# Decoder with two cross attentions: parts of 112 and 336 columns ahead of each, a fourth token buffer, token splits in other chunks

## The reference

```python
x = ln(x + linear_attn(x))                        # layer 0
def mha(x, y):                                    # 16 heads of 32
    q = ln(x) @ wq; k = ln(y) @ wk; v = ln(y) @ wv
    a = softmax(q @ k.T * 32 ** -0.5)             # causal mask for the self attention only
    x_out = x + (a @ v) @ li1_w + li1_b
    return x_out + gelu(ln(x_out) @ li2_w + li2_b) @ li3_w + li3_b
def xattn(x, ctx):
    x = ln(x); x = x + mha(x, x); x = ln(x)       # "self attention", first MLP
    return x + mha(x, ctx)                        # "first cross attention", second MLP
x = ln(x + xattn(x, ctx)); x = ln(x + fp6_linear(x))
x = ln(x + memory_block(x))                       # layer 1; ends in a third MLP with silu
x = ln(x + cross_attn(x, ctx))                    # "second cross attention", 16 heads of 8, biased
x = ln(x + moe(x))
```

## Time and profile before

| | us |
|---|---|
| median of 3 runs | 697.91 (696.05 to 698.76) |
| the profiled execution, its own time | 696.02 |
| its span in the trace | 694.2 |
| PE busy | 642.1 (92%) |
| DVE busy | 500.0 (72%) |
| ACT busy | 336.9 (49%) |
| POOL busy | 340.4 (49%) |
| granted TensorE clock, mean | 0.999 |

### The profile page before, as it was taken

The page is one execution under the profiler, slowest core; times in us unless marked ns, Lnnn a source line. Parts: engine busy times, 40 slices in busy tenths (PEclk is TensorE's granted clock), DMA queues, the critical chain, the costliest instruction groups (busy, mean ns, idle before and its releaser), DMA issues.

```text
span 694.2 us, 20149 instructions
## 1 busy us (share of the span) xinstructions
PE 642.1 (92%) x8946; PEld 483.4 (70%) x8946; DVE 500.0 (72%) x815; ACT 336.9 (49%) x503; POOL 340.4 (49%) x256
## 2 busy tenths in 40 slices
PE   8788987999999999999998888899999999998997
PEld 4576785677777777777776567567777777776774
DVE  3666733888888888887465761878988988888443
ACT  2153465066456456454354337076466465464443
POOL 1351363087696696664220313066776766845400
PEclk9999999999999999999999999999999999999999
DMA  9600003000000000000030000000000000000000
GB/s 263 225 1 2 3 2 128 1 2 2 3 2 2 2 2 2 3 2 2 2 130 22 0 1 1 1 2 2 2 2 2 2 2 2 3 2 1 3 1 13
DMA packets 3506, 14.74 MB, mean 21 GB/s; under 512 B 372, under 2 KB 628, under 8 KB 3420
## 3 DMA queue, kind: packets, MB, share of 16 engines
q1 hardware_dynamic: 3420, 13.46, 5.8%
HBM read 13.23 MB, written 0.23 MB: 19 GB/s over the span
## 4 chain that ended last, share of the span: by engine, by line
PE 66%; DVE 13%; ACT 9%; POOL 6%; issue 4%; DMA 1%; POOLq 0%; DVEq 0%; ACTq 0%
PE psum L911 16%; PE psum L820 8%; PE psum L869 5%; PE psum L198 5%; PE psum L862 5%; DVE scratch L997 4%; PE psum L864 4%; POOL scratch L982 3%; PE psum L802 1%; PE psum L826 1%; PE psum L811 1%; PE psum L667 1%; POOL nrm L1079 1%; ACT scratch L942 1%; PE psum L672 1%
## 5 line engine op out<-in xcount | busy, mean ns | idle before, releaser
L982 POOL TENSOR_TENSOR scratch<-scratch 125x896 bf16<-125x896 f32 x136 | 232.4, 1720 | 133.0 <-ACT scratch L970 132.5
L970 ACT ACTIVATE scratch<-psum 125x896 f32<-125x896 f32 x192 | 174.0, 918 | 192.5 <-PE psum L911 190.7
L997 DVE TENSOR_REDUCE scratch<-psum 128x1 f32<-128x500 f32 x336 | 210.6, 672 | 16.9 <-PE psum L820 8.5
L911 PE MATMUL psum<-scratch 128*125 128x448 bf16 (+1 forms) x768 | 177.2, 355 | 4.0 <-issue 3.7
L820 PE MATMUL psum<-scratch 128*128 128x500 bf16 x336 | 126.2, 376 | 4.9 <-ACT scratch L945 3.0
L911 PEld LDWEIGHTS psum<-scratch 128*125 128x125 bf16 (+1 forms) x768 | 97.3, 136 | 34.6 <-issue 4.3
L862 PE MATMUL psum<-tok,scratch 125*128 125x65 bf16 x1344 | 109.0, 195 | 1.8 <-DVE kT L1042 1.8
L864 PE MATMUL psum<-tok,scratch 125*128 125x64 bf16 x1344 | 108.4, 192 | 0.0
L862 PEld LDWEIGHTS psum<-tok,scratch 125*128 125x128 bf16 x1344 | 95.6, 97 | 14.0 <-issue 2.6
L864 PEld LDWEIGHTS psum<-tok,scratch 125*128 125x128 bf16 x1344 | 90.4, 99 | 14.4
L198 PE MATMUL psum<-w_second 128*128 128x256 bf16 x712 | 94.3, 272 | 0.0
(11 more groups left out here) (293 smaller groups left out, 803.0 us busy)
## 6 DMA issues: line engine op xcount, KB each, us to landing
raw<-ctx_dram SPq DMA_DIRECT2D x4, 672.0 KB
w_third<-fifth_dram SPq DMA_DIRECT2D x3, 636.0 KB, 5.2
w_third<-third_dram SPq DMA_DIRECT2D x2, 844.0 KB, 21.2
w_third<-third_dram SPq DMA_DIRECT2D x2, 843.5 KB, 19.4
w_fourth<-fourth_dram SPq DMA_DIRECT2D x3, 542.5 KB, 6.1
w_first<-first_dram SPq DMA_DIRECT2D x1, 996.0 KB, 4.9
w_second<-second_dram SPq DMA_DIRECT2D x1, 834.0 KB, 7.0
w_third<-fifth_dram SPq DMA_DIRECT2D x1, 636.5 KB, 8.4
```

The costliest lines, as they stand in the source:

```text
L911: mm = nc.tensor.matmul(bank(S + f, HALF, CP), lhs[0:rows, CP * c:CP * c + CP], rhs[0:rows, HALF * f:HALF * f + HALF], start=(rows == 128) ...
L970: nc.scalar.activation(CR["p"][0:CP, n % RING, :].rearrange("p (f n) -> p f n", f=2), psum[0:CP, S:S + 2, 0:HALF], ACT.Exp).then_inc(self. ...
L982: ops.tensor_tensor(CR["pl"][0:CP, n % RING, :], CR["p"][0:CP, n % RING, :], p_high(n % RING), ALU.subtract).then_inc(done, 1)
L997: nc.vector.tensor_reduce(mxp[:, r, t:t + 1], bank(B, TB), X_AXIS, ALU.max).then_inc(self.aux_freed, 1)
```

## The change

**Parts.** For the norms and MLPs ahead of the cross attentions (norms 3, 4, 5 and 10, 11) the two parts are 112 columns (two batches) and 336 columns. The streams are woven anew: the small part goes ahead through MLP, norms and queries; the front of the cross attention (Q and the 21 M of batch 0, which need only the first 56 columns) starts from it; the large part's last norm and its four query matmuls are put between the M units. The queries of the small part are copied by one ACT and one DVE instruction (four, two each, in the second attention) and not by four ACT copies of 448 columns. The keyed queries are read from PSUM once by ACT and once by DVE, and copied to the other 64 partitions by DVE. The transposes and copies of batch 0's tokens (T) stand ahead of the MLP's norm, in both attentions.

**Self attention.** Of the constant matmuls ahead of the last pair's transposes (30) and outputs (16), 4 and 0 are left. The scaling of the key weights on POOL goes ahead of the self attention.

**Context.** The square of lot 2 goes ahead of the exponentials, the one of lot 3 and its sum into chunks 3 and 5 of the first cross attention's batch 0.

**Tokens.** Four buffers; a batch's two lots are split in chunk 11 and in the next chunk 0. The room comes from a `qx` that now lies in `nrm`, and from squares in `w_first`.

The core of the diff:

```diff
+TOKENS = 4
+        LEAD = (slice(0, 2 * SEQ), slice(2 * SEQ, N))
         def parts_of(k):
-            return HALVES
+            return LEAD if k in (3, 4, 5, 10, 11) else HALVES
...
-                keep_warm((6, 30)[p == 3], 7)
+                keep_warm((6, 4)[p == 3], 7)
...
-                keep_warm(WARM_D if p < PAIRS - 1 else 16, 7)
+                keep_warm(WARM_D if p < PAIRS - 1 else 0, 7)
...
+            def lead_pe(self, pe, up, down, h, ready, centre, variance):
...
+                pe.wait_ge(*ready[0])
+                ups(0, range(4))
+                pe.wait_ge(*ready[1])
+                ups(1, (0, 1))
+                downs(0, range(4))
+                ups(1, (2, 3))
+                centre()
+                downs(1, (0, 1))
+                variance()
+                downs(1, (2, 3))
...
             def run_pool(self, pool):
                 for n in range(CHUNKS * BATCH):
                     b, c = n // CHUNKS, n % CHUNKS
                     if low_on_pool(n):
                         self.low_part(pool, nc.gpsimd, n, self.low_pool)
-                    if c in (1, 2) and b < BATCH - 2:
+                    if c == 0 and b < BATCH - 2:
+                        if b == 0:
+                            self.split_tokens(pool, 2, 0)
+                        self.split_tokens(pool, b + 2, 1)
+                    if c == CHUNKS - 1 and b < BATCH - 3:
                         if b:
                             pool.wait_ge(self.pv_done, CHUNKS * b)
-                        self.split_tokens(pool, b + 2, c - 1)
+                        if self is cross1 and b == 1:
+                            pool.wait_ge(cx_rstd, 2)
+                        self.split_tokens(pool, b + 3, 0)
...
         def _(act):
...
+            cross2.tokens_act(act)
             ln_act(act, 10, xo, both(m_dve, "y"))
             mlp3.run_act(act, "up_b", ACT.Silu, "silu_and_others")
-            ln_act(act, 11)
-            cross2.tokens_act(act)
+            sq_act(act, 11, 0)
+            rstd_act(act, 11, 0)
             act.wait_ge(bq_scaled, 1)
-            queries_act(act, 8.0 ** -0.5, q3, q3_act, bias=True)
+            lead_queries_act(act, 8.0 ** -0.5, q3, q3_act, True)
+            sq_act(act, 11, 1)
+            cross2.front_high_act(act)
+            rstd_act(act, 11, 1)
+            rest_queries_act(act, 8.0 ** -0.5, q3, q3_act, True)
...
         def _(pe):
...
+            lead_queries_pe(pe, "a2_wq", xn, both(ln_b, "xn"), q2)
...
+            cross1.front_pe(pe, q2_act, q2_dve, {
+                ("Q", 1): [lambda: cen_pe(pe, 5, 1, xa, both(ln_b, "xb"))], ("M", 1): [lambda: var_pe(pe, 5, 1)],
+                ("M", 7): [rest(0)], ("M", 9): [rest(1)], ("M", 11): [rest(2)], ("M", 14): [rest(3)]})
```

More of the change, by code:

```diff
@@ L216, in var, with cen_pe, var_pe @@
             return bank(VAR[p], width(parts_of(k)[p]))
+        def cen_pe(pe, k, p, x, ready):
+            pe.wait_ge(*ready[p])
+            nc.tensor.matmul(cen(k, p), par("center"), x[:, parts_of(k)[p]], start=True, stop=True
+                             ).then_inc(ln_cen[p], 1)
+        def var_pe(pe, k, p):
+            pe.wait_ge(ln_sq[p], k + 1)
+            nc.tensor.matmul(var(k, p), par("mean"), sq[:, parts_of(k)[p]], start=True, stop=True
+                             ).then_inc(ln_var[p], 1)
         def ln_pe(pe, k, x, ready):
@@ L221, in ln_pe @@
                 pe.wait_ge(loaded["second"], 16)
-            for p, cols in enumerate(parts_of(k)):
-                pe.wait_ge(*ready[p])
-                nc.tensor.matmul(cen(k, p), par("center"), x[:, cols], start=True, stop=True).then_inc(ln_cen, 1)
+            for p in PARTS:
+                cen_pe(pe, k, p, x, ready)
             if k:
@@ L229, in ln_mean, with centered @@
         def ln_mean(pe, k):
-            for p, cols in enumerate(parts_of(k)):
-                pe.wait_ge(ln_sq, 2 * k + p + 1)
-                nc.tensor.matmul(var(k, p), par("mean"), sq[:, cols], start=True, stop=True).then_inc(ln_var, 1)
+            for p in PARTS:
+                var_pe(pe, k, p)
             if k != 13:
                 keep_warm(WARM2)
-        centered = [0]
+        def centered(k):
+            return k + 1 - (k >= 9) - (k >= 10)
         def tables(name):
@@ L767, in freed, with home @@
             def freed(self, idx):
-                return sum(u[0] not in "TN" for u, _ in self.order[:idx + 1])
+                return sum(u[0] not in "TN" and (u[0], b) != ("Q", 0) for u, b in self.order[:idx + 1])
+            def home(self, idx):
+                kind, k = self.order[idx][0]
+                if idx >= len(FRONT):
+                    return SIDE[idx % 3]
+                return 4 + k if kind in "TQ" else (0, 6, 4)[(idx - 4) % 3]
             def wait_freed(self, eng, idx):
@@ L1063, in run_dve @@
                         decay_dve(dve)
+                    if self is cross1 and n == 5:
+                        context_var(dve, 3)
                     for unit in units:
```

392 lines of the change are left out of this document (259 added, 133 removed).

## The result

The changed kernel takes 690.21 us (median of 4 runs, 686.46 to 691.70), the kernel before, on the same chip, 697.63 (4 runs, 696.05 to 698.76): the ratio is 0.9886, 95% interval 0.9849 to 0.9924, so it is 1.1% faster, and the interval leaves out 1. Its profiled execution took 686.46 with a span of 684.7, against 696.02 and 694.2: the span is 9.5 us shorter.

What follows compares the result with a forecast made beforehand. PE bounds cross-attention batches; a PE, ACT, DVE chain bounds the dense stretch before the first. 9.3 + 1.9 + 3.7 - 5.6 = 9.3 us off 696.0: 686.7 profiled, 688.5 median, range 685.5 to 691.5 (wider: 682 to 694).

Steps and rivals of the forecast that it cites:

- Terms 1 and 2: Self attention's end 4.4 us earlier; from first MLP to first M, 11.2 us earlier with those 4.4 included.
- Term 3: First front: the large part's norm 5 and four query matmuls between M units pay back 1.9 us.
- My sign for a wrong term: First front: if its M units take over 15 us, the 1.9 us paid back there is wrong.
- Term 4: First cross attention's body: moved splits gain 2.5 us, the moved context sum costs 0.6; gain 1.9 us.
- Term 5: Ahead of the second cross attention: first M 5.1 us earlier, less what is paid back; gain 3.7 us.
- Term 6: Second cross attention's body: POOL's moved splits hold up L1010, 1.13 us at each of five batch ends; 5.6 us lost.
- the clock falls: Rival: fewer constant matmuls let PE's clock drop from 84 to 110 us, +20 to 708 us; chance 0.04.
- POOL doesn't stop L1010: Rival: no loss in the second cross attention's body, so 683 us; chance 0.19.
- The fronts give half: Rival: late hand-overs on ACT or DVE, so the fronts give 8 us, not 13; 693.5 us; chance 0.18.
- No change to speak of: Rival: L1010 stopped and fronts that give a third, 4 of the 13 us; 697.5 us; chance 0.07.

Runs made afterwards that it cites:

- rest_thin: Changed kernel with the first front's four query matmuls of the large part cut from 336 to 16 columns; one run, 691.25 us.
- best_lean: Changed kernel with x1_back, wait_back's order (second attention only), sum_ahead, tok2_early, and fewer constant matmuls in both fronts; 677.27 us, 0.9716 of the kernel before.
- wait_back: Changed kernel with both attentions' splits in chunks 1 and 2, each lot again waiting for the batch before; 685.44 us, 0.9827 of the kernel before.
- x1_back: Changed kernel with the first cross attention's splits back in chunks 1 and 2, without the wait; 689.48 us, 0.9891 of the kernel before.
- tok2_early: Changed kernel with T of the second cross attention moved into the memory block; 685.53 us, 0.9847 of the kernel before.
- psum_input: Changed kernel with the second cross attention's second DVE shift instruction reading PSUM, leaving out rounding and adding back the bias; one run, 687.58 us.
- sum_ahead: Changed kernel with lot 3's square and sum right ahead of the first cross attention's chunks; 688.49 us, 0.9872 of the kernel before.
- x2_back: Changed kernel with the second cross attention's splits back in chunks 1 and 2, without the wait; 685.18 us, 0.9821 of the kernel before.
- warm_back: Changed kernel with 30 and 16 constant matmuls back in the self attention's last pair; 694.57 us, 0.9953 of the kernel before.
- before_again: The kernel before, unchanged, in a second profiled execution; 697.47 us.

## Why the prediction was right, term by term

**Terms 1 and 2** (4.4 and, together, 11.2): measured 4.56 and 11.5. Each hand-over came within 0.9 us of where it was drawn: last projection 87.91 (88.5), the square behind the table load 99.39 (100.3), first M 109.57 (110.2), 0.55 us of each the earlier start of that execution. One source of this gain the terms don't name. In the kernel before, the bias step of two norms on the chain (L632, 0.34 us at 98.46) took 0.84 at 97.22 and 0.79 at 107.65, while POOL worked. At 107.65, DVE and POOL:

```profile
107.65 0.79 DVE L632 TENSOR_SCALAR xa<-t,w_second 128x224 f32<-128x224 f32 x1
```

```profile
107.41 0.90 POOL L1083 TENSOR_TENSOR tok<-nrm,tok 125x384 bf16<-125x384 f32 x1
```

In the changed kernel the small part's step takes 0.28, and POOL's last instruction there ended at 100.3. By these rows some 0.9 us (an estimate, 0.84 and 0.79 less twice 0.34) were POOL holding DVE and not the size of the parts; no run tried it apart.

**Term 3** (1.9 paid back): 2.5. The parts were mis-sized, in both directions. DVE's norm, which I counted whole at 1.1, costs 0.9; the four query matmuls, of which I exposed 0.8, cost 1.16 (rest_thin); and the mean matmul, which the term leaves out, costs 0.38 of waiting. The reason, as I read it: with three constants ahead of every M, PE needs 0.54 us where DVE needs 0.60, so PE doesn't build the lead over three banks that I let it have, and what stands between two M units shows. best_lean takes constants away just there and gets 1.5 us back. My sign for a wrong term, M units of over 15 us, lies on the line: DVE's maxima take 14.9, and from PE's first M it is 15.3.

**Term 4** (gain 1.9): 1.55, and the step behind it failed in part. "POOL does them while it had nothing to do" is true of POOL and leaves out DVE: the lots now lie beside two of DVE's low parts in chunks 0 and 1, and a batch takes 25.98, not 25.84. That the places of the splits made POOL late before was wrong too: the wait for the batch before did (wait_back against x1_back). The splits' gain was 2.2 before the sum's cost, where I had 2.5, and it came from another cause than the one given: in that the 1.9 was luck. The fourth buffer was worth 0.6 us a batch, and moving the lots took half of that away. The context sum cost 0.65, as said (0.6).

**Term 5** (gain 3.7): 3.6, from 5.2 up to the first M (5.1) and 1.6 paid back (1.4). tok2_early confirms the disputed item, T's copies ahead of the square: 1.85 for 1.5.

**Term 6** (5.6 lost): 5.1, five ends at 1.02 instead of 1.13. The term's own times don't fit each other by 0.15: it lets POOL's differences end at 502.6 and 504.2 and sets L1010 free at 502.45 and 504.05; measured, L1098 ends 0.28 and 0.21 behind POOL's differences. The mechanism is shown by two runs from two sides: POOL away from the place (wait_back) brings 0.42 and 0.35 back, and an input in PSUM (psum_input) makes the instruction deaf to POOL. The Trainium skill, "SBUF — State Buffer", section "Who interferes with whom", says that DVE with two SBUF inputs contends with a GpSimd instruction that reads SBUF, and that with at most one SBUF input it does not, outside the 2-port perf modes. The runs agree on the first, for one partition of bf16 as well: 0.42 to 0.76 with two, 0.69 and 0.69 with one in SBUF and one in PSUM. The prediction took both pairs of the earlier trace rows for cases of two SBUF inputs; the scaling at 181.13 has one, so it bears out no more than that an instruction of another kind was held too. L1098 was forecast from the first pair alone, and rightly.

**The sum and the median.** On the profiled execution the sum said 686.7 and it took 686.46. That this is so close is luck in part: the stretches gave 9.0 of the 9.3, with misses of up to 0.6 in both directions, and 0.5 came from the start of that execution. The median came out 690.21 where I had added before's 1.9. The changed kernel's four other runs, with mean clocks of 0.990 to 0.994, took 689.4 to 691.7, the one at 0.999 took 686.5; the kernel before's runs at 0.992 took 696.4 to 702.2 and those at 0.999 from 695.8 to 696.2. The falls come in both kernels; in the changed one they seem to cost more. Why is open. The traces give a price for three of the places, each against the same stretch of the changed kernel's trace: near 340 us 1.0 (sum_ahead), near 400 us 1.25 (x2_back), in the last 20 us 1.7 (warm_back). The start is another matter: x2_back reached the self attention's last masking 2.1 us later than the changed kernel (80.70 against 78.64) with a fall near 20 us, but rest_thin 2.0 later without one, psum_input 0.2 earlier with one, and before_again, with one, 0.8 earlier than the first trace of its kernel. So the start varies by some 2 us, and the fall there doesn't explain it. The rival "the clock falls" is not what happened: between 84 and 110 us no trace shows one, though 42 constants are gone, and warm_back's clock is no better.

**The rivals.** "POOL doesn't stop L1010" is refuted by the rows above. "The fronts give half" is refuted: terms 1 to 3 and 5 gave 12.5 of 13. "No change to speak of" needed both fronts to fail.

## What to carry to other kernels

A move that frees one engine has to be priced on the engine that it can hold up: before a POOL instruction goes into "idle" time, look which DVE instructions without an input in PSUM stand there (those with two SBUF inputs first of all), and whether the last ones before a hand-over are among them. The same edit was worth 0.3 us a batch in one attention and cost 1.0 in the other, since the one ends its batch on a read of PSUM and the other on an SBUF pair. When a buffer is added, try it first with the wait gone and the work where it is, and look what starts earlier by it: in the first attention the wait was the cost (0.6 us a batch), in the second it had kept POOL away from a held instruction, and without it a batch took 0.34 more. And where filler matmuls pace a stretch, real matmuls put between them can show although the engine seems to have slack: here 1.16 us of four.

## What was not expected of the hardware

- A DVE instruction on a single partition is held for the rest of POOL's, like a wide one: with 512 bf16 elements 0.42 us alone, 0.76 and 0.77 beside POOL's difference; with 384 elements 0.35 alone and 1.05.
- The holding goes both ways. POOL's cast takes 0.51 us alone and 0.71 behind a held L1098; in the first attention 1.25, and POOL's low part 2.53 instead of 1.68 beside DVE's.
- A scaling of 128x4 in fp32 with one SBUF input and none in PSUM takes 0.66 us and ends with POOL's low part, in every trace; one of the same kind and size, later in the same kernel, takes 0.17; the bias step of a norm was held in the same way, above.
- In executions of this kernel and its variants the granted clock fell for some microseconds near 20, 75, 340, 405 us or in the last 20, in one to four of these places an execution, to 0.64 over 5 us at the lowest (warm_back, 20 to 25 us), with mean clocks from 0.987 to 1.000, and the time does not follow from the mean clock alone: see the kernel before at 0.992, above.
